# Local layers: unscaled queries, their inverse lengths as the exponential's scale, and a new order of tasks

## What is computed

```python
q, k, v = jnp.split(shift_token(x) @ wqkv, 3, axis=-1)      # 8 heads of 64
q = l2norm(q) * qs
k = l2norm(k) * ksc
q, k = rotary_xpos(q, k)
sim = jnp.where(mask, -big, einsum(8.0 * q, k))             # windows of 64, own and previous
o = softmax(sim) @ v
x = x + o @ wo
h = (h - mu) / sqrt(var + 1e-5) * lg + lb                   # h = shift_token(x)
x = x + (a * gelu(g)) @ w2 + b2                             # a, g = split(h @ w1 + b1)
```

## Time and profile before

| | |
|---|---|
| median of three runs | 2219.2 us |
| the profiled execution | 2221.09 us, of which its span is 2219.4 us |
| PE busy | 2010.5 us (91%) |
| DVE busy | 1806.2 us (81%) |
| ACT busy | 1623.4 us (73%) |
| POOL busy | 1380.4 us (62%) |
| mean granted TensorE clock | 0.959 of full speed |

### The profile page before, as it was taken

The page is one execution under the profiler, slowest core; times in us unless marked ns, Lnnn a source line. Parts: engine busy times, 40 slices in busy tenths (PEclk is TensorE's granted clock), DMA queues, the critical chain, the costliest instruction groups (busy, mean ns, idle before and its releaser), DMA issues. The chain is left out here.

```text
span 2219.4 us, 52419 instructions
## 1 busy us (share of the span) xinstructions
PE 2010.5 (91%) x20476; PEld 1350.0 (61%) x20476; DVE 1806.2 (81%) x3455; ACT 1623.4 (73%) x3312; POOL 1380.4 (62%) x2090
## 2 busy tenths in 40 slices
PE   2999999999995489999999999999999999999971
PEld 1566666666663366676676676666666666666641
DVE  1788988888883468889989889896998998998746
ACT  1577777777774368888888888786878888888745
POOL 3598888888875665556556556554655655665403
PEclk9899999999998589999999999999999999999985
DMA  1001010010100111100100100111010011011014
GB/s 42 1 16 30 16 30 16 16 30 16 30 11 10 42 33 33 35 19 19 36 19 19 36 19 19 30 38 29 19 32 22 19 30 24 19 28 26 19 39 114
DMA packets 50548, 59.92 MB, mean 27 GB/s; under 512 B 8145, under 2 KB 43393, under 8 KB 48257
## 3 DMA queue, kind: packets, MB, share of 16 engines
q1 hardware_dynamic: 50304, 56.58, 10.2%
HBM read 17.90 MB, written 8.39 MB: 12 GB/s over the span
## 5 line engine op out<-in xcount | busy, mean ns | idle before, releaser
L982 POOL TENSOR_TENSOR b_part_b<-b_raw,b_tabs 128x256 f32<-128x256 f32 x512 | 432.3, 876 | 297.3 <-ACT b_raw L1041 262.7
L991 POOL TENSOR_TENSOR b_qk<-b_qk,b_part_b 128x1024 f32<-128x1024 f32 x128 | 332.2, 2596 | 271.1 <-DVE b_qk L1141 263.9
L1141 DVE TENSOR_TENSOR b_qk<-b_raw,b_tabs 128x512 f32<-128x512 f32 x256 | 296.7, 1199 | 0.1
L1242 PE MATMUL b_work<-b_w_high,b_h_high 128*128 128x512 f32 x384 | 191.1, 498 | 30.6 <-DVE b_h_low L1131 19.2
L473 POOL TENSOR_SCALAR_AFFINE_SELECT a_probs<-a_probs 128x256 f32<-128x256 f32 x512 | 203.3, 409 | 0.0
L1316 PEld LDWEIGHTS b_work<-b_v_even,b_pT 128*64 128x64 f32 x2048 | 136.9, 138 | 78.1 <-issue 72.6
L584 DVE TENSOR_REDUCE a_qpack<-a_pa 128x2 f32<-128x1024 f32 (+2 forms) x128 | 143.7, 1122 | 44.0 <-PE a_pa L655 41.4
L1062 ACT ACTIVATE b_probs<-b_sb,b_neg_max 128x128 f32<-128x128 f32 x512 | 147.9, 383 | 41.4 <-DVE b_neg_max L1163 41.0
L422 POOL TENSOR_TENSOR a_idle<-a_idle 128x1 f32<-128x1 f32 x432 | 86.6, 200 | 146.9 <-ACT a_probs L516 85.2
L1030 ACT ACTIVATE b_sq<-b_work 128x1024 f32<-128x1024 f32 x128 | 131.7, 1029 | 54.4 <-PE b_work L1244 43.7
L1068 ACT COPY b_pT<-b_work 128x512 f32<-128x512 f32 x256 | 154.4, 603 | 23.0 <-PE b_work L1306 23.0
(11 more groups left out here) (211 smaller groups left out, 5518.1 us busy)
## 6 DMA issues: line engine op xcount, KB each, us to landing
b_v_even<-b_v SPq DMA_DIRECT2D x32, 528.0 KB, 4.4
b_v_even<-b_v SPq DMA_DIRECT2D x32, 396.0 KB, 5.8
a_x_in<-in_L_attn_x SPq DMA_DIRECT2D x16, 256.0 KB, 3.2
a_x_again<-in_L_attn_x SPq DMA_DIRECT2D x16, 256.0 KB, 3.5
x_scratch<-a_x SPq DMA_DIRECT2D x16, 256.0 KB, 2.5
out<-c_y SPq DMA_DIRECT2D x4, 1024.0 KB, 5.4
b_w_raw<-in_L_ffn_wqkv SPq DMA_DIRECT2D x2, 768.0 KB, 4.3
b_tabs<-tab SPq DMA_DIRECT2D x2, 512.0 KB, 4.2
```

Source lines behind the costliest of these rows:

```text
L982: last = pool.tensor_tensor(part_b[:, x, :].rearrange("p (h d) -> p h d", d=DH)[:, :, lo:lo + DH // 2], raw[:, i % 2, x, :].rearrange("p ( ...
L991: pool.tensor_tensor(qk[:, i], qk[:, i], part_b[:], ALU.add).then_inc(c_made, 1)
L1141: last = dve.tensor_tensor(qk[:, i, x, :].rearrange("p (h d) -> p h d", d=DH), raw[:, i % 2, x, :].rearrange("p (h d) -> p h d", d=DH), ta ...
L1242: pe.matmul(x, h_high[:, t], w_high[:, cols], start=True, stop=False)
```

## The change

Queries are no longer multiplied by their inverse lengths. `scale` now does keys alone, 128x512 for a tile, and keeps its place behind rope_add; `turn_q` waits for rope_add itself (c_made), `turn_k` for `scale`. The inverse lengths of the queries, kept in a buffer of two slots, go to the exponential as its `scale` operand, one number for a partition. The row maximum must then be multiplied too: row_max writes `raw_max`, waits for it, and a product of 128x8 makes `neg_max`. POOL's h waits until the last projection is written (filled) and no longer until ACT has read it. The table ORDER is another.

```diff
-OWN_STEPS = {"newton": 3, "divide": 1, "variance": 2, "rstd": 3, "weights_ffn": 1}
+OWN_STEPS = {"newton": 3, "row_max": 1, "divide": 1, "variance": 2, "rstd": 3, "weights_ffn": 1}
...
-        ss, seed, rs, tmp = (sb(n, [P, TT * 2 * HEADS]) for n in ("ss", "seed", "rs", "tmp"))
+        ss, seed, tmp = (sb(n, [P, TT * 2 * HEADS]) for n in ("ss", "seed", "tmp"))
+        rs = sb("rs", [P, 2, TT, 2, HEADS])
+        raw_max = sb("raw_max", [P, PAIRS, 2, TT])
...
-                    ready(freed[which], fills + 1)
+                    ready(filled[which], fills + 1)
...
-                                          bias=neg_max[:, slot, h, i:i + 1])
+                                          bias=neg_max[:, slot, h, i:i + 1], scale=rs[:, slot, i, 0, h:h + 1])
...
-                a = qk[:, i].rearrange("p x (h d) -> p (x h) d", d=DH)
-                dve.tensor_tensor(a, a, rs[:, i * 16:(i + 1) * 16].rearrange("p (h a) -> p h a", a=1).to_broadcast([P, 16, DH]),
+                a = qk[:, i, 1].rearrange("p (h d) -> p h d", d=DH)
+                dve.tensor_tensor(a, a, rs[:, slot, i, 1, :].rearrange("p (h a) -> p h a", a=1).to_broadcast([P, HEADS, DH]),
                                   ALU.mult).then_inc(scaled, 1)
...
-                dve.tensor_reduce(neg_max[:, slot, 2 * p:2 * p + 2, :], bank_of[which][:].rearrange("p a (i k) -> p a i k", i=TT),
-                                  AX, ALU.max, negate=True).then_inc(maxed, 1)
+                step = steps("row_max", p, l, b)
+                step(dve.tensor_reduce(raw_max[:, p], bank_of[which][:].rearrange("p a (i k) -> p a i k", i=TT), AX, ALU.max, negate=True))
+                dve.tensor_tensor(neg_max[:, slot, 2 * p:2 * p + 2, :], raw_max[:, p],
+                                  rs[:, slot, :, 0, 2 * p:2 * p + 2].rearrange("p i a -> p a i"), ALU.mult).then_inc(maxed, 1)
...
             def turn_q(l, b, i, slot):
-                pe.wait_ge(scaled, seq(l, b) * TT + i + 1)
+                pe.wait_ge(c_made, seq(l, b) * TT + i + 1)
...
             def turn_k(l, b, i, slot):
+                pe.wait_ge(scaled, seq(l, b) * TT + i + 1)
...
-    (1, "turn_k", 1, "w0"), (2, "copy_p", 5), (2, "p_turn", 6, "w1"), (1, "turn_q", 2, "o"), (1, "copy_k", 1),
...
+    (2, "p_turn", 5, "w0"), (2, "divide", 2), (1, "rope_add", 3), (2, "copy_p", 5), (1, "turn_k", 1, "w1"),
...
```

More of the change, by code:

```diff
@@ new lines @@
+    (0, "square_sums", 1), (1, "exp", 0), (2, "divide", 6), (0, "project_k", 2, "w1"), (2, "divide", 7),
+    (1, "row_max", 1), (0, "rope_sin", 1), (0, "square", 2), (1, "exp", 1), (2, "out", 0, "o"), (2, "o_turn", 3, "x"),
+    (2, "out", 1), (2, "copy_o", 3), (2, "out", 2), (1, "p_turn", 0, "x"), (0, "rope_cos", 1), (0, "square_sums", 2),
+    (0, "raw_q", 2), (1, "copy_p", 0), (0, "raw_k", 2), (2, "out", 3), (2, "residual", 0), (0, "project_v", 0, "w0"),
+    (0, "rope_cos", 2), (0, "project_v", 1, "x"), (1, "exp", 2), (0, "copy_v", 0), (0, "rope_add", 1),
@@ new lines @@
+    (0, "project_k", 3, "w1"), (0, "copy_v", 1), (0, "project_q", 3, "w0"), (2, "stat_turn", 0, "x"),
+    (1, "p_turn", 1, "o"), (1, "exp", 3), (0, "square", 3), (1, "scores", 2, "sb"), (0, "raw_q", 3), (0, "raw_k", 3),
+    (0, "rope_sin", 2), (1, "scores", 3, "sa"), (1, "copy_p", 1), (2, "variance", 0), (1, "values", 0, "o"),
+    (0, "square_sums", 3), (2, "rstd_seed", 0), (1, "values", 1, "x"), (2, "rstd", 0), (0, "project_v", 2, "w1"),
+    (2, "rstd_turn", 0, "w0"), (1, "divide", 0), (0, "copy_v", 2), (1, "p_turn", 2, "o"), (2, "normalise", 0),
@@ new lines @@
+    (0, "limit", 0), (1, "copy_p", 2), (0, "project_v", 3, "w1"), (2, "gate", 0, "w0"), (2, "gate", 1, "o"),
+    (0, "seed", 0), (1, "row_max", 2), (0, "copy_v", 3), (1, "divide", 1), (2, "gelu", 0), (0, "newton", 0),
+    (2, "gelu", 1), (2, "hidden", 0, "w1"), (0, "scale", 0), (2, "gate", 2, "x"), (1, "p_turn", 3, "w0"),
+    (2, "product", 0), (2, "hidden", 1, "o"), (2, "gelu", 2), (1, "copy_p", 3), (1, "exp", 4), (2, "hidden", 2, "x"),
+    (0, "scale", 1), (2, "product", 1), (0, "turn_q", 0, "w0"), (0, "turn_q", 1, "o"), (2, "down", 0, "w1"),
@@ L788 @@
+    (2, "down", 1), (1, "exp", 5), (2, "product", 2), (2, "down", 2), (0, "copy_q", 1), (0, "copy_q", 0),
+    (1, "p_turn", 4, "o"), (1, "copy_p", 4), (0, "rope_cos", 3), (0, "turn_k", 0, "x"), (0, "rope_add", 2),
+    (0, "scale", 2), (0, "turn_q", 2, "w0"), (0, "rope_sin", 3), (0, "shift_v", 0), (1, "values", 2, "o"),
+    (0, "copy_k", 0), (2, "result", 0), (1, "o_turn", 0, "x"), (0, "copy_q", 2), (1, "copy_o", 0),
 ]
```

11 lines of the change are left out of this document (10 added, 1 removed).

## The result

The changed kernel takes 2222.5 us (median, 2221.1 to 2224.4), the kernel before 2219.2: a ratio of 1.0014, interval 1.0008 to 1.0021. The interval does not hold 1: the kernel is slower, by 0.14%, which is less than the 0.2% that the prediction took as the least change to be told from none. The time lies in the stated range, but the forecast of 2193 us, 1.2% faster, did not come.

A forecast was written before the change was run, and what follows sets the result against it. PE was taken as the bound, at 98% of an ordinary step. Terms of -0.8 - 1.1 + 0.9 gave -1.0 us a step, -29 us over 29 steps, and +3 at the ends: 2193 us median, range 2168 to 2240.

The forecast's parts named there:

- The wait of stat_turn: PE's wait at stat_turn for DVE's residual, 0.79 us each, disappears in the new order: -0.8 us a step.
- Fewer changes of kind: PE's tasks form 29 runs of one kind instead of 43; fourteen fewer at 0.08 us: -1.1 us a step.
- The second operand: ACT's exponential gets dearer, 3.0 us of ACT a step; PE waits for part of it: +0.9 us a step.
- the three places that the prediction named: PE close behind exponentials: p_turn 6 and 7, scores 2, p_turn 4; 0.3 us of wait at each.
- The lock of DVE by POOL: Rival: rstd's or row_max's small DVE products last as long as POOL's instruction; 1.4 to 2.2 us a step; chance 0.26.
- ACT takes the gain back: Rival: PE's waits behind dearer exponentials cost about 1.9 us a step, no net gain, 2219 to 2222 us; chance 0.15.
- Hidden exponential: Rival: ACT's idle 7.5 us a step hides all the dearer exponential; -1.9 us a step, 2167 us; chance 0.17.
- Turn_q and h, priced at nothing: Turn_q without scale and h behind filled shorten chains PE does not wait for in an ordinary step: no gain.
- DVE 1.4 us lighter: In each step scale saves 2.2 us of DVE and row_max's product adds 0.8; not a gain by itself.
- The ends, +3: Last step, fill and drain: row_max 3, exp 6 and dearer exponentials without projections to hide them; 3 us once.
- PE's busy time a step 1 us or more lower: Sign that the forecast is right: PE's busy time falls this much, since the changes of kind lie in it.

The follow-up runs named there:

- one_operand_pool_waits: The changed kernel with a constant as the exponential's scale, queries' inverse lengths left out, and POOL's rope_add 2 starting only when rstd is done; 2158.2 us, ratio 0.9722.
- two_operands: The kernel before, with its exponential given a second operand that holds ones; 2223.0 us, ratio 1.0012.
- the bar: An added wait: POOL starts rope_add 2 only when rstd is done; on the changed kernel 2203.9 us, ratio 0.9930.

## Why the prediction was wrong

*The wait of stat_turn, -0.8.* Right: it is gone, in every run with the new order. By the starts it was worth more: in the kernel before, stat_turn starts 1.75 us after project_v 1, a projection that takes 0.80 where nothing waits.

*Fewer changes of kind, -1.1.* Right. Before, a step without that wait is 41.69 - 0.79 = 40.90 us; one_operand_pool_waits, whose PE has no gap, takes 39.72. The 1.18 us between them, over 14 changes, would be 0.084 us each, against the 0.08 taken. That is a remainder, and both kernels have further small waits in it. An estimate without them, from the starts in the PE timelines: with each task at the shortest distance to the next that a run shows for its kind between the same neighbours, a step takes 40.20 us in the old order and 39.00 in the new, 0.086 us for each change. The order's gain is 1.97 us by the steps, where 1.9 was forecast; that the two come so close is partly luck, since by this estimate each of the two kernels loses 0.7 us a step in waits that neither term counts.

*The second operand, +0.9, the weakest number.* Too small: by itself it is 1.43 us, and 1.00 beside POOL's lock. The duration was right: 0.48 to 0.51 us for one. It is paid at the three places that the prediction named, by 0.4 us ahead of scores 0, 0.2 at scores 2 and 0.55 at p_turn 4, where it said 0.3 each. It is also paid at two that it did not name, 0.3 us at p_turn 0 and 0.4 at project_q 3 and the stat_turn behind it, which wait for copies that stand behind an exponential on ACT. Together that is more than 1.43, since one_operand_pool_waits loses 0.5 us of its own.

*The lock of DVE by POOL: the step that failed.* It stood among the rivals, priced at 1.4 to 2.2 us, and the sum held nothing for it. It came: 0.55 us a step beside the operand (41.70 - 41.15), 0.98 without it. The error was to treat it as an alternative: forecast and rival name different engines and do not exclude each other. The step came out 1.0 us longer than forecast, 41.70 against 40.7. Counted beside the operand, the lock is 0.55 of it, the operand's wrong size 0.53, and the order gives 0.07 back; counted the other way round, the lock is 0.98 and the operand 0.10. So the lock is half of the miss or more, and the operand's size the rest. That -0.79 - 1.18 + 1.00 + 0.98 = 0.01 adds up to the step of after is no test, since 1.18 is a remainder of the same steps. The rival's price was too high as well: with it the step would have been 0.4 to 1.2 us longer than before. The prediction had the place (rstd behind rope_add 2) and the length of the add in hand, and let a chance of 0.26 stand for a term. Which product would suffer it had only half right: row_max's is nearly free in this order, 0.17 us in the median, 0.6 at most, and costs 1.87 us in the old one.

*ACT takes the gain back.* Its time came, 2222.5 us beside 2219 to 2222, but by luck: ACT takes 1.0 to 1.4 of the 1.97 us, and POOL the rest.

*Hidden exponential.* Wrong here, yet in the old order it is fully hidden (two_operands). The slack of ACT, 7.5 us a step in the earlier trace rows, said nothing on either; what decided were 11.3 us of the step in which ACT has hardly a gap.

*Turn_q and h, priced at nothing.* Right for the whole, since neither kernel waits at the turns in an ordinary step. It hides that the new order, with the bar, waits 1.4 us a step there when queries are scaled.

*DVE 1.4 us lighter.* It is 2.30. rope_cos, not in that sum, is the rest: 943 ns on average against 1225 before in the same step, 8 x 0.28 = 2.3, less the products held by POOL. It lies less beside POOL now: 6.2 us of it run while POOL is in an instruction, and 8.3 did before.

*The ends, +3.* The median is 3.3 us up with equal steps. In the profiled runs the last sequence begins 3.7 us earlier (2045.48 against 2049.19) and the span ends 1.5 us later, so the drain costs 5.2. The fill and the steps that are not ordinary give 3.7 back. Near the 3 us of the prediction, that is a difference of two terms that it did not have.

*What would show it.* "PE's busy time a step 1 us or more lower" was a bad sign: it fell by 0.26 us, while PE could do the same work in 39.72. Part of a wait lies inside what the profile calls busy, so the step against a kernel without the wait, or the distances between the starts of tasks, tell more than the busy time.

## What to carry to other kernels

Add the rivals that can come true together before you choose between them: two mechanisms on different engines at different places of a step are two terms, which may overlap (by 0.43 us here), and only those on the same gap are alternatives. When a tiny chain of DVE is on the path, look at which long POOL instruction it can fall under, and let POOL wait for it if POOL has slack (2.2 us of waiting here cost nothing and gave 0.55 us a step, 0.98 without the second operand; in the kernel before, where no such chain lay under the add, the same bar gave nothing). The slack of an engine over a step does not hide a dearer instruction; look for the stretch in which that engine has no gap, and for what the bound engine needs out of it.
